# Adding an attention mask on TensorE instead of seeding it by ScalarE, in every fourth step

## The reference, cut to what matters

```python
adj = jnp.maximum(adjacency_matrix, eye)
scores = jnp.einsum('hqk,hmk->hqm', q, k) * kd ** (-0.5)
scores = scores + IDENTITY_BIAS * eye - MASK_VAL * (1.0 - adj)
att = jax.nn.softmax(scores, axis=-1)
return jnp.einsum('hqm,hmk,hko->qo', att, v, Wo)
```

## Time and profile before

| | us |
|---|---|
| median of 3 runs | 4965.33 (4965.26 to 4973.84) |
| profiled execution, its own time | 4967.11 |
| profiled execution, span | 4965.3 |
| second attention, first to last exponential | 2566 to 4778 |
| TensorE busy, whole span | 4163.5 (84%) |
| VectorE busy | 3641.2 (73%) |
| ScalarE busy | 3633.4 (73%) |

### The profile page before, as it was taken

One profiled execution on the slowest core, in us unless ns is written; L12 is line 12 of the kernel. 1 busy time (PEld: TensorE's weight loads), 2 busy tenths in 40 slices (PEclk: granted clock), 3 DMA queues, 4 the chain that ended last, 5 costly groups with the idle time before them and its releaser, 6 DMA issues. The chain is left out here.

```text
span 4965.3 us, 106706 instructions
## 1 busy us (share of the span) xinstructions
PE 4163.5 (84%) x42500; PEld 2761.3 (56%) x42500; DVE 3641.2 (73%) x6026; ACT 3633.4 (73%) x4642; POOL 343.2 (7%) x527
## 2 busy tenths in 40 slices
PE   7922239988998999699749999999999999999977
PEld 4412228888888898444315555555555555555543
DVE  1245559999999999622258888888888888888834
ACT  1133349999999999411139999999999999999952
POOL 0000000000000000000010202011120202111000
PEclk9955559999999999899969999999999999999999
DMA  1299994444444444344453635444353535444223
GB/s 63 86 305 362 355 339 148 162 165 152 149 162 162 155 149 161 105 149 156 138 140 91 167 87 143 103 126 122 93 164 86 160 88 147 111 116 130 68 72 144
DMA packets 413632, 742.27 MB, mean 149 GB/s; under 512 B 90040, under 2 KB 282744, under 8 KB 376184
## 3 DMA queue, kind: packets, MB, share of 16 engines
q1 hardware_dynamic: 349296, 643.60, 43.0%
q0 software_dynamic: 20608, 75.51, 4.7%
q10 hardware_dynamic: 43280, 16.92, 1.3%
HBM read 567.42 MB, written 168.49 MB: 148 GB/s over the span
## 5 line engine op out<-in xcount | busy, mean ns | idle before, releaser
L1186 DVE CUSTOM_DVE_ANT_0 m_junk<-m_rough,m_rows 128x1024 bf16<-128x1024 f32 x1024 | 1253.6, 1224 | 304.7 <-PE m_rough L1053 236.7
L671 PE MATMUL g_acc<-g_vals,g_pos 128*128 128x130 f16 (+1 forms) x8192 | 1201.1, 250 | 128.7 <-DVE g_neg L626 102.0
L552 ACT ACTIVATE g_step<-g_arow,g_steep 128x512 bf16<-128x512 f32 x2048 | 1258.4, 711 | 58.5 <-DVE g_neg L626 38.2
L1135 ACT ACTIVATE m_scores<-m_strip 128x1024 f32<-128x1024 bf16 x1024 | 1053.0, 1028 | 103.4 <-POOL m_strip L984 39.7
L1149 ACT ACTIVATE m_whole<-m_scores 128x1024 int32<-128x1024 f32 x1024 | 1037.7, 1013 | 83.9 <-DMA scr_offset<-m_offset 35.8
L1067 PE MATMUL m_acc<-m_v,m_halves 128*128 128x129 f16 (+1 forms) x16384 | 901.8, 208 | 49.4 <-ACT m_got L1112 49.4
L671 PEld LDWEIGHTS g_acc<-g_vals,g_pos 128*128 128x128 bf16 x8192 | 811.5, 99 | 207.0 <-DVE g_neg L626 104.4
L1067 PEld LDWEIGHTS m_acc<-m_v,m_halves 128*128 128x128 f16 x16384 | 754.9, 98 | 286.4 <-issue 189.8
L1081 PE MATMUL m_scores<-m_qA,m_kA 128*128 128x512 f16 x2048 | 786.2, 384 | 33.1 <-ACT m_scores L1135 33.0
L1086 PE MATMUL m_scores<-m_qB,m_kB 65*128 65x512 f16 x2048 | 784.9, 383 | 0.0
L1211 DVE TENSOR_SCALAR m_halves<-m_whole 128x2048 f16<-128x2048 uint16 x1024 | 708.6, 692 | 80.2 <-ACT m_whole L1149 73.1
(11 more groups left out here) (146 smaller groups left out, 3161.3 us busy)
## 6 DMA issues: line engine op xcount, KB each, us to landing
g_vals<-scr_gat_v SPq DMA_DIRECT2D x128, 1040.0 KB, 5.3
m_v<-scr_v SPq DMA_DIRECT2D x64, 1032.0 KB, 7.3
b_stage<-in_adj SPq DMA_DIRECT2D x64, 1024.0 KB, 9.8
m_kA<-scr_k_hi SPq DMA_DIRECT2D x128, 512.0 KB, 6.1
scr_row_mask<-b_rowm SPq DMA_DIRECT2D x64, 512.0 KB, 8.7
scr_no_edge_T<-b_colm SPq DMA_DIRECT2D x64, 512.0 KB, 8.3
g_strip<-scr_no_edge_T SPq DMA_DIRECT2D x64, 512.0 KB, 7.6
m_kB<-scr_k_lo SPq DMA_DIRECT2D x64, 512.0 KB, 5.4
```

The source lines that it names most:

```text
L552: ins = nc.scalar.activation(step[:, j % RING, t, :], arow[:, b, :], ACT.Sigmoid, scale=STEEP, bias=steep[:, b, 2 * j + t:2 * j + t + 1])
L671: mm = pe.matmul(acc[:, b, it, lo:hi], edges, vals[:, b, 2 * j + t, lo:hi], start=j == 0 and t == 0 and lo == 0, stop=j == PAIRS - 1 and t ...
L1135: nc.scalar.activation(scores[:, n % 2], strip[:, 2 * st:2 * st + 2, :].rearrange("p t i -> p (t i)"), ACT.Copy, scale=-BIG / 2).then_inc( ...
L1186: nc.vector.tensor_tensor_reduce(out=junk[:, n % 2], in0=rough[:].rearrange("p a m -> p (a m)"), in1=rows[:, n % TC, n // TC * WIDE:(n // ...
```

## The change

In the steps with `st % 4 == 3`, ScalarE issues no seed. Instead TensorE starts the accumulation afresh with its first product, and adds to each of the two key tiles one product of 512 columns with a constant: the identity times -2^55 (`negbig`) against the tile of `strip`. In such a step TensorE no longer waits for a seed but for the exponential of two steps before, which reads the same PSUM tile, and for the piece of `strip`. GpSimd's reload of `strip` waits for the lower count of seeds, and besides for the scores of the steps that read the piece.

```diff
+            nc.vector.tensor_scalar(k.negbig[:], k.identf[:], -BIG / 2, None, ALU.mult)
...
+        def seeds_before(u, st):
+            return 3 * STEPS // 4 * u + 3 * (st // 4) + min(st % 4, 3)
...
-                    pool.wait_ge(seeded, STEPS * (H * c - 1) + 2 * (g + 1))
+                    pool.wait_ge(seeded, seeds_before(H * c - 1, 2 * (g + 1)))
+                    pool.wait_ge(scored, STEPS * (H * c - 1) + 2 * (g + 1))
...
-                pe.wait_ge(seeded, STEPS * u + st + 1)
+                on_seed = st % 4 != 3
+                if on_seed:
+                    pe.wait_ge(seeded, seeds_before(u, st) + 1)
+                else:
+                    pe.wait_ge(exped, STEPS * u + st - 1)
+                    pe.wait_ge(strip_in[st // 2], 16 * (unit_chunk(u) + 1))
...
-                    pe.matmul(to, kA[:, u % KSLOTS, m * P:(m + 1) * P], qA[:, b, :], start=False, stop=False, skip_group_check=True)
+                    pe.matmul(to, kA[:, u % KSLOTS, m * P:(m + 1) * P], qA[:, b, :], start=not on_seed, stop=False, skip_group_check=True)
+                    if not on_seed:
+                        pe.matmul(to, k.negbig[:], strip[:, m, :], start=False, stop=False, skip_group_check=True)
...
-                    if STEPS * u + st + 2 < U * STEPS:
+                    if STEPS * u + st + 2 < U * STEPS and (st + 2) % 4 != 3:
                         seed(STEPS * u + st + 2)
...
+        k.negbig = s.sb("negbig", [P, P], BF16)
```

## The result

| | median us | runs |
|---|---|---|
| before | 4964.85 | 6 (4960.44 to 4973.84) |
| after | 4991.14 | 6 (4988.23 to 4996.18) |

The ratio is 1.0054, with a 95% interval of 1.0041 to 1.0067: the change makes the kernel slower, by 26 us between the medians (20 to 33 by the interval). Forecast were 50. The profiled execution after has a span of 4987.3 us, 22.0 above the one before.

The account below looks back on a forecast made before the run. TensorE was taken to set the pace at 2.02 us a plain step. Masks +81.6, offset -26 and tail -6 sum to +49.6 us on 4965.3, so 5015 us, range 4985 to 5047.

Parts of the forecast that it names:

- the cure of all long units: Bound on the offset's gain: the last two units of each chunk lose all their 52.6 us excess; range's lower edge 4988.
- The pace is TensorE's: Second attention's plain steps: TensorE's starts leave no gap, 2.02 us a step, so added products are paid unless something waits.
- (1): Steps with st % 4 = 3: two more products cost TensorE 0.434 us each; 250 such steps remain before the tail.
- (2): Step 3 of 62 units: mask free inside the wait for the accumulator's copy; 188 masks paid, +81.6 us.
- (3): ScalarE issues 256 seeds less, 1.03 us each; some 4.1 us a unit turn idle, buying nothing in plain units.
- (4): Last two units of each chunk: the offset's store leaves about 1.2 us sooner, shortening waits: -26 us.
- The cover: Time from the offset's store to its load that costs nothing: 1.5 us more in each long unit.
- The clock: Long units: two stalls become too short to halve TensorE's granted clock, some 2.4 us each.
- The landing: Offset's store to load in long units: no shortening counted; 9.78 us is more than 1.5 us of cover can hide.
- (5): Last 24 steps, without L1053, where ScalarE is back to back: -1 us per four steps, -6 us together.
- The feared upper bound of (4): GpSimd's later strip pieces could meet the offset's store on the DMA engines: seven units lose 3 us more, +20.

Follow-up runs that it names:

- experiment 1: Kernel before, all seeds kept, two extra products of 512 columns (constant of zeros) in steps with st % 4 = 3, strip released later: 5020.62 us, ratio 1.0117.
- experiment 2: Changed kernel without the mask products, so every fourth step has neither seed nor mask: 4918.27 us, ratio 0.9912.
- experiment 3: Changed kernel with the change kept in step 3 of each unit alone, the other steps keeping their seeds: 4950.19 us, ratio 0.9977.
- experiment 6: Kernel before, with the stores of result and offset issued behind the exponential of step 9 instead of behind the seed of step 11: 4924.6 us, ratio 0.9936.
- experiment 7: Changed kernel with both stores issued one step later, ahead of the exponential of step 11 instead of step 10: 5054.99 us, ratio 1.0197.
- experiment 8: Kernel of experiment 6 (early stores), with the load of the offset moved from step 12 to step 13: 4912.12 us, ratio 0.99.
- experiment 9: Kernel before, with only the load of the offset moved from step 12 to step 13, the store in its old place: 4927.41 us, ratio 0.9935.
- experiment 5: Kernel before, with GpSimd's strip pieces waiting for the scores as well as the seeds, nothing else changed: 4960.46 us, ratio 1.0.
- experiment 4: Changed kernel with the even strip pieces released by the seeds alone, without the wait for scores: 4995.28 us, ratio 1.0075.
- experiment 10: Kernel of experiment 8, with the accumulator's copy moved from behind the seed of step 4 to behind the exponential of step 2: 4878.26 us, ratio 0.9831.
- experiment 11: Kernel of experiment 10, with the mask of step 3 made by products and no seed there: 4891.96 us, ratio 0.9861.

## Why the prediction was right, and where it was off

The direction came out for the reasons given, and four of the five terms came out near their size. The time is in the range, but 6 us above its lower edge, and the slowdown is about half of what was forecast: one term, the offset, is worth nearly twice what it was put at. The range held because its lower edge took in the cure of all long units, a bound that the prediction named and did not expect.

*The pace is TensorE's.* Right, by experiments 1 and 2: the unit gets longer by the three masks that nothing hides and does not move when 4 us of ScalarE's work go. What told was the constant 0.31 us from the last score product to M. The Trainium skill's rule ("Perfetto Trace Analysis", section "Identifying the Most-Contended Engine": judge TensorE's headroom by achieved rate and weight loads, ScalarE by occupancy) would have chosen ScalarE, at 96%; experiment 2 does not agree with it. But the prediction worked out only the weight loads' 55%. The rate was much nearer to full. An estimate: at 0.217 us for 512 columns, a step's products (16 of 129 columns and two of 512 at full height, four of 512 at about half) make 1.75 of its 2.02 us, 86%.

*(1) and (2), the masks.* Right in size: 2.45 us in steps 7, 11 and 15, 2.34 in step 4 instead of 2.78, units of 35.04, +80.6 us in the table where +81.6 was forecast. (33.74 is the length of a plain unit before; the median of the 63, which the prediction names for it, is 33.76.) Step 3 was free, as experiment 3 shows by itself.

*(3), ScalarE's freed time.* Right for plain units: it turned into waiting, 331 us in all. That it also makes the long units shorter was missed (see (4)).

*(4), the offset.* This is the term that was mis-sized: -26 forecast, -46.5 measured. The mechanism, an earlier store and more cover, held in experiments 6 to 9. One thing was misread: the prediction counted the 63rd unit's 2.0 us as an offset that came late. The offset was there in time (3.74 us from store to load), and what that unit lost is the lower clock behind the wait for the copy, shown above. The rest is three sizes.

The cover was to grow by 1.5 us and grew by 2.0. Before, a unit loses what its store to load is over 4.7 (5.8 cost 1.1, 6.7 cost 1.9); after, what it is over 6.7 (7.2 cost 0.5, 7.5 cost 0.8). The store's move gave 1.15 (1.48 us behind M of step 9 before, 0.33 after, as the median) and the mask of step 11 0.43, both as forecast. The other 0.4 is ScalarE's freed time. Experiments 2 and 6 differ in it: in both the store stands 0.33 us behind M and a plain unit lasts 33.75 us, but with all seeds the cover is 5.9 (7.2 cost 1.3), and without every fourth it is 6.2 (7.4 cost 1.2).

The clock was to give two stalls of 2.4 us. In the trace before, six long units show the lower clock (15, 23, 31, 38, 47 and 55) and lose 1.1 to 2.6 us more than the cover explains, 13.3 together; in the trace after, no unit does.

The landing I held unchanged. It shortened in the last units of a chunk, from 7.0 to 9.9 us down to 3.8 to 7.5; in the seventh units it did not (5.8 to 7.5 before, 6.4 to 7.6 after). GpSimd's loads and the store's landing in unit 15 (each last line is from the view of the tile `scr_offset` over that stretch), before:

```profile
3095.81 3.25 POOL L969 DMA_DIRECT2D m_strip<-scr_no_edge_T  x4
...
DMA to landing us min/median/max: 9.8/9.8/9.8
```

And after:

```profile
3109.05 3.68 POOL L973 DMA_DIRECT2D m_strip<-scr_no_edge_T  x4
...
3109.58 0.52 ACTq L1128 DMA_DIRECT2D scr_offset<-m_offset  x1
...
3114.89 0.24 ACTq L1132 DMA_DIRECT2D m_qB<-scr_offset  x1
...
DMA to landing us min/median/max: 3.8/3.8/3.8
```

GpSimd issues four pieces of the strip in a row, 512 KB each. Before, the store of 1 KB came 2.90 us behind the first of them (3098.71) and landed after 9.8 us; after, it came 0.53 us behind and landed after 3.8. The load stands 5.31 us behind the store because ScalarE comes to it only then. So a short landing goes not with an early store as such but with few large loads issued shortly before it. In the seventh units the loads of `rows` stand there, two of them 2.2 and 1.4 us ahead of the early store in experiment 6, and it landed later than before (7.1 to 8.2 us); the late store of experiment 7 has the last of them 4.7 us or more ahead and landed after 3.6 to 4.8. That the store queues behind the loads' packets fits; which queue or engine it is was not tried.

An estimate of the three parts, from the 14 long units' times from store to load: 2.0 us more cover with the old landings is worth 25 us (21 forecast), the clock 13 (5 forecast), the shorter landings 8 (nothing forecast). They hang together. In experiment 9, with landings as long as the old ones and a cover of 6.8, the two longest stalls still reached the lower clock.

*(5), the tail.* -6 forecast, -6.4 measured (-5.6 in the 63rd unit and -0.8 in the last steps). That they agree is in part luck: 2.4 us of it are the lower clock in the kernel before. In experiment 5, which has every seed and the same wait of 1.84 us for the copy, the granted clock stays at 1.00 behind it and the 63rd unit takes 33.35 us.

The feared upper bound of (4), GpSimd's later release, did not show (experiments 4 and 5).

## What to carry to other kernels

Before work is moved off an engine with a high busy share, look whether some other engine's starts follow each other without a gap: that one sets the pace, and each instruction added to it is paid in full except where it stands ahead of a wait. Such a wait is then better removed than filled (experiment 10 against 11). And a small store that is read back on the critical path should leave ahead of a burst of large loads, not behind it, and be waited for late; here moving the stores and the load (experiment 8) gave 49 us, nearly twice what the change cost.

## What was not expected of the hardware

A store of 1 KB took 2.6 to 9.9 us to land in the kernel before, 3.7 as the median, and it mattered what had been issued ahead of it: 0.5 instead of 2.9 us behind the start of a burst of 2 MB, it had landed after 3.8 instead of 9.8 us. Stalls of TensorE cost more than their length: in six units of the kernel before, 1.1 to 2.6 us more, at a granted clock of 0.50. And products with bf16 operands between products in fp16 kept the same 0.22 us from start to start.
